# An audio tower's expert stage: steps without a loop, transposing loads, wider limit and product, one rank sum per step

## The reference

```python
g = t @ gate_w.T + gate_b                 # t: normed token, 192 values
vals, idx = jax.lax.top_k(g, K)           # K = 4 of E = 16 experts
w = jax.nn.softmax(vals, axis=-1) / K
h = jnp.einsum('th,ehf->tef', t, w1) + b1 # 192 -> 2 x 192
h = _swiglu(h)   # min(glu, 7) * sigmoid(1.702 * min(glu, 7)) * (clip(lin, -7, 7) + 1)
y = jnp.einsum('tei,eih->teh', h, w2) + b2
out = jnp.einsum('teh,te->th', y, full_w) * K
```

## Time and profile before

| What | us |
|---|---|
| median of three executions | 790.51 |
| the profiled execution's own time | 788.26 |
| its span in the profile | 786.5 |
| expert stage, first transpose to last second product | 545.2 to 739.3 |
| TensorE busy over the span | 408.7 (52%) |
| VectorE busy | 624.7 (79%) |
| ScalarE busy | 546.8 (70%) |
| GpSimd busy | 437.5 (56%) |

### The profile page before, as it was taken

One profiled execution on the slowest core, in us unless ns is written; L12 is line 12 of the kernel. 1 busy time (PEld: TensorE's weight loads), 2 busy tenths in 40 slices (PEclk: granted clock), 3 DMA queues, 4 the chain that ended last, 5 costly groups with the idle time before them and its releaser, 6 DMA issues. The chain is left out here.

```text
span 786.5 us, 16017 instructions
## 1 busy us (share of the span) xinstructions
PE 408.7 (52%) x4141; PEld 279.9 (36%) x4142; DVE 624.7 (79%) x1844; ACT 546.8 (70%) x914; POOL 437.5 (56%) x542
## 2 busy tenths in 40 slices
PE   0377545553434444544534332322999999999400
PEld 0123213232222232322312222211777777878300
DVE  3686478989599598796995988775998888888378
ACT  0235289998878788778788876426998899889300
POOL 9543263735417558378287386774366566666600
PEclk9999655555555555555555555555999999999655
DMA  8479999688201102002000001123344443333095
GB/s 185 52 166 321 319 318 296 200 264 258 60 1 39 58 24 72 25 24 85 11 24 30 29 5 49 64 79 90 94 126 122 118 121 111 108 114 98 3 380 209
DMA packets 102400, 93.47 MB, mean 119 GB/s; under 512 B 14822, under 2 KB 96493, under 8 KB 102338
## 3 DMA queue, kind: packets, MB, share of 16 engines
q1 hardware_dynamic: 88938, 72.87, 33.5%
q0 software_dynamic: 10272, 17.70, 6.5%
q10 hardware_dynamic: 3128, 2.16, 0.9%
HBM read 35.21 MB, written 61.24 MB: 123 GB/s over the span
## 5 line engine op out<-in xcount | busy, mean ns | idle before, releaser
L686 POOL DMA_INDIRECT expert_rows<-stage,dest x118 | 116.3, 985 | 85.8 <-DVE dest L1414 64.8
L622 POOL DMA_INDIRECT region<-rows,slots x60 | 65.4, 1090 | 17.8 <-issue 14.0
L1486 PE MATMUL pX<-arena,WA 128*128 128x384 f16 x86 | 35.3, 514 | 66.2 <-ACT arena L771 63.5
L537 POOL TENSOR_TENSOR w1s<-stage,w1s 128x384 f16<-128x384 f32 (+8 forms) x72 | 56.4, 784 | 9.6 <-ACT w1s L744 4.6
L1593 PE MATMUL pP<-idb,S_p 128*88 128x128 bf16 x192 | 25.8, 315 | 65.5 <-DVE S_p L1253 65.5
L1705 PE MATMUL pX<-w2s,stage 128*128 x472 | 56.8, 251 | 4.3 <-ACT stage L908 2.6
L651 POOL CAST oq<-o 128x384 bf16<-128x384 int8 x24 | 19.3, 804 | 68.7 <-ACT o L837 68.5
L1593 PEld LDWEIGHTS pP<-idb,S_p 128*88 128x88 bf16 x192 | 21.9, 191 | 70.8 <-DVE S_p L1253 68.8
L610 POOL CAST arena<-arena 128x384 bf16<-128x384 int8 x42 | 25.5, 614 | 38.1 <-ACT arena L771 37.8
L914 ACT ACTIVATE stage<-arena 128x512 f16<-128x512 f32 x59 | 37.2, 630 | 13.4 <-DVE arena L1410 12.2
L827 ACT ACTIVATE S_g<-S_w,kf 128x1056 int16<-128x1056 uint16 x24 | 30.3, 1264 | 21.6 <-DVE S_w L1227 21.6
(11 more groups left out here) (369 smaller groups left out, 1733.0 us busy)
## 6 DMA issues: line engine op xcount, KB each, us to landing
region<-zrow SPq DMA_DIRECT2D x45, 800.0 KB
arena<-region SPq DMA_DIRECT2D x59, 200.0 KB
w1s<-expert_rows SPq DMA_DIRECT2D x16, 384.0 KB, 8.0
stage<-in_L_ffn_w_dram SPq DMA_DIRECT2D x24, 192.0 KB
stage<-in_L_ffn_w_dram SPq DMA_DIRECT2D x8, 384.0 KB
w2s<-expert_rows SPq DMA_DIRECT2D x8, 384.0 KB, 13.8
arena<-in_x_dram SPq DMA_DIRECT2D x4, 672.0 KB
expert_rows<-stage,dest POOLq DMA_INDIRECT x118
```

Of the source, the lines that this page charges most:

```text
L537: pool.tensor_tensor(ws[rows, min(kind + 1, 3), two, to:to + width], st[rows, :, at:at + width], ws[rows, kind, two, to:to + width], ALU.s ...
L622: pool.indirect_dma_start(region_rows, bass.IndirectOffsetOnAxis(ap=slots[q % 3][:, i, m:m + 1], axis=0), rows[q % 3][:, i, :].bitcast(I16 ...
L686: pool.indirect_dma_start(y_dram, bass.IndirectOffsetOnAxis(ap=dest[(st - 7) % 8][:, j:j + 1], axis=0), ysb[b][:, j, :], None, bounds_chec ...
L1486: ins = pe.matmul(bank[:, 0:384], W[:, 128 * c:128 * c + 128], xT[:, kind, :], start=kind == 0, stop=kind == 2)
```

## The change

It has these parts, all in the expert stage:

- `step_slots` has no loop: 66 slots are written out. The expert words are read into registers once, not once per eight slots.
- The load of a step is a transposing DMA, which brings `region`'s 256 rows x 384 numbers as 128 partitions x 3 x 256 straight into `xTb` (now eight buffers of 16-bit numbers). The 16 tag numbers of each row come by a transfer of their own into `meta` (32 bytes per row, two neighbouring rows per partition). SyncE waits, from step 8 on, for the first product, the tail copy and the rank sum of the step eight before.
- TensorE's six transposes and ScalarE's copy of `tp_ps` are gone. ScalarE's 64-partition copy (`tEb`) stays, now from SBUF.
- Because partition p now holds tags of rows 2p and 2p + 1, the activation is written out with a stride: ScalarE's and VectorE's reads of `act_f` take every second number (`by_half`).
- `hidL` and `hidC` lie in neighbouring PSUM banks, and one `tensor_scalar` of 512 columns limits both. It waits for the third window **and for both gate functions of the same slot**.
- One `scalar_tensor_tensor` of 512 columns makes the product. The gate function of `hidC` goes to partitions 64 to 127; partitions 0 to 63 of that half are zeroed once.
- One rank comparison and one `tensor_reduce` per step take the place of two comparisons with accumulators and a cast.

```diff
-        def step_slots(eng, begin, slot):
+        def step_slots(eng, slot):
...
+            for st in range(NS + 7):
                 slot(st, st, st // UNROLL)
-            with eng.Fori(2, last) as it:
...
+        def by_half(full):
+            return full.rearrange("p k (n j) -> p k j n", j=2)
...
 # SyncE
-                if st >= 4:
-                    sp.wait_ge(s["tp_filled"], p - 3)
-                    sp.wait_ge(s["dest_ready"], p - 3)
-                sp.dma_start(xb[b], region[bass.ds(k, 1)].rearrange("o (j p) c -> p (o j) c", p=128)).then_inc(step_loaded[b], 16)
+                if st >= UNROLL:
+                    sp.wait_ge(s["hl_ready"], p - (UNROLL - 1))
+                    sp.wait_ge(s["te_copied"], p - (UNROLL - 1))
+                    sp.wait_ge(s["dest_ready"], p - (UNROLL - 1))
+                sp.dma_start(xTb[b], region[bass.ds(k, 1), :, 0:2 * C].rearrange("o n c -> (o n) c"),
+                             transpose=True).then_inc(step_loaded[b], 16)
+                sp.dma_start(meta[b], region[bass.ds(k, 1), :, 2 * C:ROW].rearrange("o (p j) c -> p (o j) c", j=2),
+                             allow_slow_non_contiguous=True).then_inc(meta_loaded[b], 16)
...
 # GpSimd, once
-            for buf in act_f:
-                pool.memset(buf[CB:128, 1, :], 0.0).then_inc(s["tails_zeroed"], 1)
+            for buf in gsig:
+                pool.memset(buf[0:CB, 1, :], 0.0).then_inc(s["tails_zeroed"], 1)
+            for buf in rkj:
+                for j in range(2):
+                    pool.memset(buf[:, j, TOPK:], -float(j)).then_inc(s["tails_zeroed"], 1)
...
 # ScalarE
                 if active(st, 3):
-                    act.wait_ge(s["a_ready"], p * 2 - 4)
+                    act.wait_ge(s["a_ready"], p - 2)
...
-                    act.activation(av[b][:, 0:3:2, :], act_f[b], ACT.Copy).then_inc(s["hi_ready"], 1)
-                    act.activation(avE[b][0:CB, :], act_f[b][0:CB, 1, :], ACT.Copy).then_inc(s["ave_ready"], 1)
+                    act.activation(av[b][:, 0:3:2, :].rearrange("p k (j n) -> p k j n", j=2), by_half(act_f[b]),
+                                   ACT.Copy).then_inc(s["hi_ready"], 1)
+                    act.activation(avE[b][0:CB, :].rearrange("p (j n) -> p j n", j=2), by_half(act_f[b])[64:128, 1],
+                                   ACT.Copy).then_inc(s["ave_ready"], 1)
...
                 if active(st, 0):
-                    act.wait_ge(s["tp_filled"], p + 1)
+                    act.wait_ge(step_loaded[u], it * 16 + 16)
...
-                    act.activation(xTb[st % 4], tp_ps, ACT.Copy).then_inc(s["tp_drained"], 1)
-                    act.activation(tEb[st % 4][0:CB, :], tp_ps[0:CB, 2, :], ACT.Copy).then_inc(s["te_copied"], 1)
+                    act.activation(tEb[st % 4][0:CB, :], xTb[u][0:CB, 1, :].bitcast(F16), ACT.Copy).then_inc(s["te_copied"], 1)
...
 # VectorE
-            dve.wait_ge(s["own_ready"], 2)
+            dve.wait_ge(s["own_ready"], 1)
+            dve.wait_ge(s["tails_zeroed"], 6)
...
                 if active(st, 2):
-                    dve.wait_ge(s["h_ready"], p * 3 - 4)
+                    dve.wait_ge(s["hl_ready"], p - 1)
+                    dve.wait_ge(s["gs_ready"], p * 2 - 2)
                     if st >= 4:
-                        dve.wait_ge(s["a_ready"], p * 2 - 6)
-                    dve.tensor_scalar(lin[r][0:CB, 1, :], hidC[r][64:128, :], -6.0 * XS * WS, 8.0 * XS * WS, ALU.max,
-                                      ALU.min).then_inc(s["l_done"], 1)
-                    dve.wait_ge(s["h_ready"], p * 3 - 3)
-                    dve.tensor_scalar(lin[r][:, 0, :], hidL[r], -6.0 * XS * WS, 8.0 * XS * WS, ALU.max,
+                        dve.wait_ge(s["a_ready"], p - 3)
+                    dve.tensor_scalar(lin[r], hidLC[r], -6.0 * XS * WS, 8.0 * XS * WS, ALU.max,
                                       ALU.min).then_inc(s["l_done"], 1)
...
-                    dve.tensor_tensor(av[g][:, 1, :], act_f[g][:, 0, :], av[g][:, 0, :], ALU.subtract).then_inc(s["lo_ready"], 1)
+                    parts, halves = av[g].rearrange("p k (j n) -> p k j n", j=2), by_half(act_f[g])
+                    dve.tensor_tensor(parts[:, 1], halves[:, 0], parts[:, 0], ALU.subtract).then_inc(s["lo_ready"], 1)
+                    dve.tensor_tensor(parts[0:CB, 2], halves[64:128, 1], parts[64:128, 2],
                                       ALU.subtract).then_inc(s["lot_ready"], 1)
...
-                    for j in range(2):
-                        ins = dve.scalar_tensor_tensor(rkj[o][:, j, :], meta[:, j, 0:TOPK], own[:, bass.ds(p - 1, 1), j],
...
+                    dve.scalar_tensor_tensor(rkj[o][:, :, 0:TOPK], tags[:, :, 0:TOPK], own[:, st - 1:st],
+                                             tags[:, :, TOPK:2 * TOPK], ALU.is_gt, ALU.add).then_inc(s["rk_done"], 1)
...
-                    for m, part in enumerate((slice(0, 128), slice(0, CB))):
-                        dve.wait_ge(s["gs_ready"], p * 2 + (m - 3))
-                        dve.wait_ge(s["l_done"], p * 2 - 2)
-                        dve.scalar_tensor_tensor(act_f[f][part, m, :], gsig[r][part, m, :], G7, lin[r][part, m, :], ALU.min,
-                                                 ALU.mult).then_inc(s["a_ready"], 1)
+                    dve.wait_ge(s["l_done"], p - 1)
+                    dve.scalar_tensor_tensor(act_f[f], gsig[r], G7, lin[r], ALU.min, ALU.mult).then_inc(s["a_ready"], 1)
...
-                    dve.tensor_copy(dest[(st - 1) % 8][:, :], rk[o][:, :]).then_inc(s["dest_ready"], 1)
+                        dve.tensor_reduce(dest[(st - 1) % 8][:, :], rkj[o][:, :, :], AX, ALU.add).then_inc(s["dest_ready"], 1)
...
 # TensorE
-                    for j in range(2):
-                        for kind, lo in enumerate((0, 2 * CA, CA)):
-                            ins = pe.transpose(tp_ps[:, kind, 128 * j:128 * j + 128], xb[b][:, j, lo:lo + 128].bitcast(F16), idh[:, :])
-                    ins.then_inc(s["tp_filled"], 1)
```

More of the change, by code:

```diff
@@ L245, in audio_tower @@
         tabi = sb("tabi", [128, 2, 80], I32)
-        own = sb("own", [128, 64, 2], F32)
+        own = sb("own", [128, 64], F32)
         packf = sb("packf", [128, 16, 4], F32)
@@ L472, in load_step @@
             def load_step(st, p, it):
-                b = st % 4
+                b = st % UNROLL
                 if st >= NS:
                     return
-                k = sp.value_load(tabi[0:1, 1, bass.ds(p + 8, 1)], min_val=0, max_val=NBLK)
-                if st >= 4:
-                    sp.wait_ge(s["tp_filled"], p - 3)
-                    sp.wait_ge(s["dest_ready"], p - 3)
-                sp.dma_start(xb[b], region[bass.ds(k, 1)].rearrange("o (j p) c -> p (o j) c", p=128)).then_inc(step_loaded[b], 16)
-            step_slots(sp, lambda it: None, load_step)
+                _, (k,) = nc.values_load_multi_w_load_instructions(
+                    tabi[0:1, 1, st + 8:st + 9], [mybir.EngineType.SP], min_val=0, max_val=NBLK,
+                    skip_runtime_bounds_check_because="the table's column of rows is held below by zero and above by NBLK")
+                if st >= UNROLL:
[6 more added lines that the diff above has]
+                             allow_slow_non_contiguous=True).then_inc(meta_loaded[b], 16)
+            step_slots(sp, load_step)
             for b in range(4):
@@ L1649, in _ @@
             pe.matmul(tab_ps, ones_h[:, :], tdiag[:, :, :], start=True, stop=True).then_inc(s["tabs_spread"], 1)
-            pe.wait_ge(s["own_ready"], 2)
+            pe.wait_ge(s["own_ready"], 1)
             pe.wait_ge(s["tabs_ready"], 2)
             pe.wait_ge(s["stage_low"], 12 * E // 2)
-            words = [None, None]
-            def load_experts(it):
-                _, values = nc.values_load_multi_w_load_instructions(
-                    packw[0:1, bass.ds(it, 2)], [mybir.EngineType.PE],
-                    skip_runtime_bounds_check_because="each of the eight fields of four bits is cut out before it is used")
-                words[:] = values
@@ L1663, in expert @@
-            def expert(u, lag):
-                word, field = (words[1], u - lag) if u >= lag else (words[0], u - lag + UNROLL)
-                return (word >> (4 * field)) & (E - 1)
+            _, words = nc.values_load_multi_w_load_instructions(
+                packw[0:1, 1:9], [mybir.EngineType.PE],
+                skip_runtime_bounds_check_because="each of the eight fields of four bits is cut out before it is used")
+            def expert(n):
+                return (words[n // 8] >> (4 * (n % 8))) & (E - 1)
@@ L1675, in products @@
                         pe.wait_ge(s["gs_ready"], p * 2 - 6)
-                    k_ = expert(u, 2)
-                    x3, tail = xTb[(st - 2) % 4], tEb[(st - 2) % 4]
+                    k_ = expert(st - 2)
+                    x3, tail = xTb[b].bitcast(F16), tEb[(st - 2) % 4]
                     for window, dst in enumerate((hidG[r], hidC[r], hidL[r])):
```

(4 more changed lines are left out.)

87 lines of the change are left out of this document (35 added, 52 removed).

## The result

The kernel after takes 856.0 us (median of 4 runs, 854.0 to 856.94), the kernel before 790.77 us in runs beside them (4 runs, 790.07 to 792.04). The ratio is 1.082, with a 95% interval of 1.0795 to 1.0844. The profiled execution took 854.0 us with a span of 852.3.

The account below looks back on a forecast made before the run. TensorE bounded the kernel before; afterwards a VectorE-ScalarE circle of 3.9 us per slot would. 56 x (3.9 - 3.1) = +45, minus 5 for beginning and end, gave 830 us; range 820 to 845 (72%), extended to 864.

Parts of the forecast that it names:

- the circle of waits: VectorE and ScalarE, once per slot: limit, product, next slot's high part, gate functions, next limit; 3.9 us per slot.
- ScalarE's part: Two high-part copies and two gate functions on the circle, 0.54, 0.30, 0.27 and 0.36 us: 1.47 us per slot.
- Hops: Handovers between the engines on the circle: 0.03 us to ScalarE, 0.06 back to VectorE.
- The transposing load: Load of each expert step: up to 1.5 us plus 0.75 for tags, 2.3 us, hidden in a 3.9 us slot.
- The beginning: Start of the expert stage: first limit at about 549, next two slots 3.2 and 3.0 us, slot 4's limit at 555.3.
- The end: After the last product: no GpSimd scatter backlog with a slower pipeline, about 8 us left, 3.5 us less than before.
- The circle is longer by strides or hops: Rival, 10%: upper bounds make the circle 5.65 us; a stride's cost on VectorE alone makes 4.4, giving 858 us.
- TensorE binds, about 755: Rival, 7%: gates ready when VectorE reaches its limit, slots of 2.6 to 2.8 us, 35 us gained.
- The load binds: Rival, 5%: the transposing load decides from 3.9 us per step; at 5 us per step, 895 us.
- the clock falls: Rival, 3%: TensorE, busy 67%, drops to 1.2 GHz; a slot of 5.0 us, 892 us.
- they cancel: Rival, 2%: gains and circle cancel, a slot of about 3.2 us, time within 0.3%.

Follow-up runs that it names:

- the run with the same partitions: Kernel after with ScalarE's second gate function and small high-part copy on partitions 0 to 63, not 64 to 127: 838.28 us against 791.1, ratio 1.0592.
- the run without strides: Kernel after with the activation's halves read as contiguous runs, not every second number: 852.11 us against 791.1, ratio 1.0766.
- gates first: Kernel after with ScalarE's gate functions ahead of its high-part copies: 769.04 us against 791.66; on slow chips 835.85 against 847.9 and 833.34 against 847.36.
- the kernel with the one added wait: Kernel before, with VectorE also waiting for both gate functions of the slot ahead of its first limit: 872.35 us against 847.9, ratio 1.0299.

## Why the prediction came out right, and what was off

The prediction said 830 us: 820 to 845 with a chance of 72%, extended upwards to 864. It is 856. The forecast was the circle of waits, and the circle it was. Its size was not: a slot of 4.22 us lies outside the 3.75 to 4.15 of the 72%. That 856 still lies below 864 is in part luck, since the upper piece was there for a stride's cost on one engine, and the strides cost 0.05 us. Another term filled it. In the order of its steps:

- **The circle and its members: right.** The timeline has them in the predicted order. Limit 643.48 - 642.87 = 0.61, subtractions 0.89, rank 0.15, product and hop 645.23 - 644.52 = 0.71: all four as in the sum, to 0.01 us. Taking them from operations of half the width and a slope of 1.0 ns per column held.
- **ScalarE's part: this term was mis-sized.** The prediction has 1.47 us, "ScalarE: 664.30 to 664.84 (0.54), to 665.14 (0.30), to 665.41 (0.27), and 0.36 to the end". It measured 0.70 + 0.33 + 0.41 + 0.38 = 1.82. The mistake was to carry start-to-start distances, which hold an overlap, over to operations that start at other partitions. Of the 0.35 us, by the run with the same partitions (0.57 + 0.32 + 0.26 + 0.36 = 1.51), 0.31 is the overlap that was lost; what is left is the stride, at 0.04 to 0.05 us by the run without strides. The change itself gave the sign of this: it puts the gate function of `hidC` on partitions 64 to 127.
- The Trainium skill ("VectorE: DVE Perf Modes", the section on two Vector instructions with no wait between them) has a rule of the same form: an instruction whose input or output starts in another 32-partition group than the last one in that memory starts only when all earlier ones have finished. The Trainium skill states it of VectorE alone. The two operations that lost their overlap on ScalarE agree with it, and so does the gate function that kept its own behind the copy, since its input lies in the other memory; on VectorE, so does the one in the earlier trace rows that starts 0.44 us after a 0.41 us operation (665.24 to 665.68).
- **Hops.** 0.09 back to VectorE, where 0.06 was taken. Together with ScalarE this makes 4.27 in the shown slot against 3.89. VectorE's idle time ahead of the limit, foretold as some 1.3 us, is 1.83 and 1.86 in the rows shown, and the profile names "issue" there and not ScalarE.
- **The transposing load: right that it stays hidden.** It takes longer than a plain one, 3.16 us for the first against 2.49. The queue in 40 us of the kernel after, and its issues:

```profile
q1 hardware_dynamic: 10626, 2.05, 28.7%
...
arena<-region SPq DMA_TRANSPOSE x5, 3.3
```

  These are 9 steps (5 into `arena` and 4 into tiles with names of their own), so 0.287 x 40 / 9 = 1.28 us of 16 engines per step with its tags, under the 2.3 us allowed. The rows do not separate the load from its tags. So the 261 GB/s of the Trainium skill ("DMA: Bandwidth & Descriptors", latency and other measured facts), by which the prediction had an estimate of 0.75 us for the load without tags, is neither confirmed nor contradicted.
- **The beginning: 2.6 us short.** The first limit came at 551.2, not 549: 1.1 us because the scatters ahead of the stage ended later, 0.7 from the longer load, the rest between the tail copy and the end of TensorE's windows. The next two slots took 3.35 us each, not 3.2 and 3.0, so the limit of slot 4 came at 557.9, not 555.3.
- **The end: a saving that did not exist.** The prediction read GpSimd's scatters up to 744.8 as a backlog and took 3.5 us off. It was none that a slower pipeline takes away: the last product ends at 797.6 + 0.7 = 798.3, and this is what follows:

```profile
802.23 0.49 ACT L911 ACTIVATE stage<-pX 128x384 f32<-128x384 f32 x1 [2.06 <-PE pX L1690]
...
804.78 0.49 ACT L911 ACTIVATE stage<-pX 128x384 f32<-128x384 f32 x1 [2.06 <-PE pX L1690]
805.47 0.97 POOL L689 DMA_INDIRECT expert_rows<-stage,dest  x1 [0.30 <-ACT stage L911]
...
809.31 0.97 POOL L689 DMA_INDIRECT expert_rows<-stage,dest  x1 [0.30 <-issue]
```

  Second product and evacuation alternate on the one `y_ps`, 2.55 us a round at TensorE's lower clock, then four scatters follow at 1.28 us each. That is 12.0 us from the product's end to the end of the last scatter, against 11.5 before.
- **The sum.** Slots: from slot 4 to slot 60 they took (796.1 - 557.9) / 56 = 4.25 us, (4.25 - 3.9) x 56 = 19.8 us more than predicted. Beginning 2.6, end 4.3. Together 26.7, and 829.6 + 26.7 = 856.3.
- **Rivals.** "The circle is longer by strides or hops" was right in its outcome, 4.4 us for 858, but not by its mechanism: the stride cost 0.05 us. "TensorE binds, about 755" fell, yet it tells what the kernel is without the circle: 769. In that kernel a slot of TensorE was 2.74 and not 2.6 us, and SyncE's two issues per step would follow closely: at the start of its stage one step's issue follows the last after 2.42 us (552.42 to 554.84). "The load binds", "the clock falls" and "they cancel" fell; TensorE was busy for 25.53 of the 40 us from 600 at a granted clock of 1.00.

## What to carry to other kernels

Two engines that work in order form a circle as soon as each waits, within one slot, for something that the other does behind its own wait. Write the slot numbers of all waits of two engines beside one another before merging two operations into one, since the merged one waits for the latest input of both; where such a circle shows, look first whether exchanging two blocks in one engine's list opens it. And where a distance between two starts is taken over as a cost, ask whether the new operations still lie in the same partitions: the overlap belongs to the pair, not to the operation.

## What was not expected of the hardware

- ScalarE starts the next operation about 0.1 us before the last one ends, but not in the pairs where input or output within SBUF moves between partitions 0 and 64. That was 0.13 and 0.15 us at two places of the circle (a third pair, the tail copy 0.40 us behind a gate function of 0.38, lies off it).
- A transposing load of 192 KB took 1.23 us to issue on SyncE and, in the median, 3.3 us to land. It used no more of the DMA engines than 1.28 us per step, tags included.
- On two chips of at least four the kernel before took 847 us, 7% more. In the expert stage of gates first VectorE and ScalarE waited there for 2 to 5 us time and again, with limits of unchanged length; in the kernel with the one added wait the slots did not lengthen.
